# Decoder kernel on one core: zero matmuls between the products of the cosine stage, another order in a step, one bank for the sums

## The chip, the cores and the metric

The kernel runs on one core of a Trainium2 chip. A core has TensorE (PE: matmuls and weight loads), VectorE (DVE), ScalarE (ACT), GpSimd (POOL) and SyncE (SP, transfers). Each works through its own list of instructions in order and waits on semaphores that others raise. TensorE writes to PSUM, eight banks of 512 float columns; VectorE and ScalarE read them there. TensorE's clock is granted at one of two levels, 1.2 or 2.4 GHz; a profile shows it as 0.5 or 1.0. The metric is the device time of one execution in microseconds (us), smaller is better.

## What is computed

Two decoder layers on x of 16 sequences x 128 rows x 128 channels and a context of 16 x 128 x 96. Each part is added to x after a layer norm of x: in layer 0 causal attention, cross attention and a mixture of experts, in layer 1 attention over the batch, a cosine similarity with the context and an MLP with blockwise FP4 quantisation. The change touches the cosine part alone:

```python
def _L1_xattn_ref(visual_features, text_features, Wv, bv, Wt, bt):
    v = jnp.einsum('bsd,hd->bsh', visual_features, Wv) + bv      # h = 64
    t = jnp.einsum('bsd,hd->bsh', text_features, Wt) + bt
    dots = jnp.einsum('bih,bjh->bij', v, t)
    vn = jnp.linalg.norm(v, axis=-1)
    tn = jnp.linalg.norm(t, axis=-1)
    denom = jnp.maximum(vn[:, :, None] * tn[:, None, :], EPS)
    return dots / denom
...
    x = x + _L1_xattn_ref(_layernorm(x, axis=-1), ctx_768, L1_xattn_Wv, L1_xattn_bv, L1_xattn_Wt, L1_xattn_bt)
```

## The kernel before

The stages follow one another as blocks, with all engines meeting between two of them: the attentions of layer 0, the experts, the attention over the batch (`batch_attention`, from about 499 us), `back_block`, which turns its result back and adds it to x (670 to 681 us), `cosine_block` (682 to 722 us) and `mlp_block` (722 us to the end). x stays in SBUF all the time. The context's side of the cosine (`M.cos_tt`, the projected context, and `M.cos_inv`, its inverse norms) was made in an earlier stage.

`cosine_block` goes through the 16 sequences in pairs: N = 8 steps, u = 0 to 7, and p = u % 2 chooses one of two buffers. For a pair:

- VectorE subtracts the mean and scales (`normalise`, L1726, tile `cos_xn`).
- TensorE turns the two 128x128 tiles (`turn`, L1643); ScalarE copies them to SBUF (`turned`, L1695, `cos_xt`).
- TensorE multiplies with the weights (`project`, L1650, 64 x 256 result, recorded as two MATMULs of 256 columns). ScalarE squares it with the bias (`biased`, L1683, `cos_sq`) and stores it with the bias (L1685, `cos_vt`).
- TensorE sums the squares with a column of ones (`sums`, L1656: two matmuls of one column, recorded as four, each with its weight load). ScalarE takes the root (`roots`, L1690, `cos_norm`), VectorE floors it and takes the reciprocal (`inverses`, L1732 and L1735), GpSimd multiplies it into `M.cos_inv` and limits it (L1715, two tiles, `cos_m`).
- TensorE makes the products with the context (`products`, L1664: two matmuls of 128 columns, recorded as four). VectorE multiplies them by `cos_m` (`cosines`, L1740), adds the result to x (`add`, L1745) and takes the statistics for the next layer norm (`statistics`, L1751 and L1754).

The order is written by hand. In one pass of TensorE's loop over u stand `project` of pair u+1, `sums` and `products` of pair u and `turn` of pair u+2; ScalarE's passes are `biased` u+1, `roots` u, `turned` u+2; VectorE's are `normalise` u+3, `cosines` u-1, `inverses` u, `add` and `statistics` u-1. The loops are written out, not run on registers. `wait(engine, semaphore, u, per, plus)` waits until the semaphore has reached per * u + plus and is left out where that is zero or less. PSUM banks 0 and 1 hold the turned tiles, 2 and 3 the projections, 4 and 5 the sums, 6 and 7 the products, by parity.

The stage begins with the scales of the layer norm for all rows: VectorE adds the epsilon (L206), ScalarE loads its table and takes the root (L214), VectorE takes the reciprocal (L208).

Of the kernel before, what the change touches and what calls it, by code (L numbers as in the profile page):

```python
# [15 lines left out]
BF16 = mybir.dt.bfloat16  # L16
I32 = mybir.dt.int32
ALU = mybir.AluOpType
ACT = mybir.ActivationFunctionType
# [24 lines left out]
def wait(eng, sem, t, per=1, plus=0):  # L44


    value = per * t + plus
    if isinstance(value, int) and value <= 0:
        return
    eng.wait_ge(sem, value)  # L50
# [20 lines left out]
def valid(t, count):  # L71

    return not isinstance(t, int) or 0 <= t < count
# [35 lines left out]
def semaphores(nc, tag, names):  # L109


    return {n: nc.alloc_semaphore(name=f"{tag}_{n}") for n in names.split()}
# [92 lines left out]
def scales_on_vector(nc, M, dve, s):  # L205
    nc.vector.tensor_scalar(M.rstd[:, :, 0], M.mv[:, :, 1], EPS_LN, None, ALU.add).then_inc(s["variance"], 1)  # L206
    dve.wait_ge(s["root"], 1)
    nc.vector.reciprocal(M.rstd[:, :, 0], M.root[:, :]).then_inc(s["rstd"], 1)  # L208
    dve.wait_ge(s["rstd"], 1)


def scales_on_scalar(nc, M, act, s):
    act.wait_ge(s["variance"], 1)
    nc.scalar.activation(M.root[:, :], M.rstd[:, :, 0], ACT.Sqrt).then_inc(s["root"], 1)  # L214
# [1400 lines left out]
def cosine_block(nc, M, d):  # L1615
# [5 lines left out]
    with ExitStack() as ctx:  # L1621
        one = lambda n, shape, dt=F32: ctx.enter_context(nc.sbuf_tensor(f"cos_{n}", shape, dt))
        two = lambda n, shape, dt=F32: [one(f"{n}{p}", shape, dt) for p in range(2)]
        s = semaphores(nc, "cos", """variance root rstd xn xt_ps xt vt_ps vt sq sum_ps norm floored inverse
            limited dot_ps cosine x_done stats aggr""")
        N = B // 2
        xn, xt = two("xn", [S, 2, D]), two("xt", [D, 2, S])
        vt, sq = two("vt", [HC, 2, S]), two("sq", [HC, 2, S])
        norm, floored, inv = two("norm", [S, 2]), two("floored", [S, 2]), two("inv", [S, 2])
        m, cosine = two("m", [S, 2, S]), two("cosine", [S, 2, S])  # L1630
        stats = [one(f"stats{j}", [S, 6]) for j in range(4)]
        turn_bank, vt_bank, sum_bank, dot_bank = M.bank[0:2], M.bank[2:4], M.bank[4:6], M.bank[6:8]
        halves = lambda t: t[:, 0:2 * S].rearrange("p (j s) -> p j s", j=2)

        with nc.Block() as block:

            @block.tensor
            def _(pe):
                def turn(u, p):
                    wait(pe, s["xn"], u, per=2, plus=2)  # L1640
                    wait(pe, s["xt"], u, plus=-1)
                    for j in range(2):
                        mm = nc.tensor.transpose(turn_bank[p][:, j * S:(j + 1) * S], xn[p][:, j, :], M.ident[:, :])  # L1643
                    mm.then_inc(s["xt_ps"], 1)

                def project(u, p):
                    wait(pe, s["xt"], u, plus=1)
                    wait(pe, s["vt"], u, plus=-1)
                    wait(pe, s["sq"], u, plus=-1)
                    nc.tensor.matmul(vt_bank[p][0:HC, 0:2 * S], M.cos_wv[:, 0:HC], xt[p][:, :, :], start=True, stop=True).then_inc(s["vt_ps"], 1)  # L1650

                def sums(u, p):
                    wait(pe, s["sq"], u, plus=1)
                    wait(pe, s["norm"], u, plus=-1)
                    for j in range(2):
                        mm = nc.tensor.matmul(sum_bank[p][:, j:j + 1], sq[p][:, j, :], M.ones[0:HC, 0:1], start=True, stop=True)  # L1656
                    mm.then_inc(s["sum_ps"], 1)

                def products(u, p):
                    wait(pe, s["vt"], u, plus=1)  # L1660
                    wait(pe, s["cosine"], u, plus=-1)
                    for j in range(2):
                        b = 2 * u + j
                        mm = nc.tensor.matmul(dot_bank[p][:, j * S:(j + 1) * S], vt[p][:, j, :], M.cos_tt[:, b * S:(b + 1) * S], start=True, stop=True)  # L1664
                    mm.then_inc(s["dot_ps"], 1)

                for u in range(-2, N):
                    if valid(u + 1, N):
                        project(u + 1, (u + 1) % 2)
                    if valid(u, N):  # L1670
                        sums(u, u % 2)
                        products(u, u % 2)
                    if valid(u + 2, N):
                        turn(u + 2, u % 2)

            @block.scalar
            def _(act):
                scales_on_scalar(nc, M, act, s)

                def biased(u, p):  # L1680
                    wait(act, s["vt_ps"], u, plus=1)
                    wait(act, s["sum_ps"], u, plus=-1)
                    nc.scalar.activation(sq[p][:, :, :], halves(vt_bank[p][0:HC]), ACT.Square, bias=M.cos_bias[0:HC, 0:1]).then_inc(s["sq"], 1)  # L1683
                    wait(act, s["dot_ps"], u, plus=-1)
                    nc.scalar.activation(vt[p][:, :, :], halves(vt_bank[p][0:HC]), ACT.Identity, bias=M.cos_bias[0:HC, 0:1]).then_inc(s["vt"], 1)  # L1685

                def roots(u, p):
                    wait(act, s["sum_ps"], u, plus=1)
                    wait(act, s["floored"], u, plus=-1)
                    nc.scalar.activation(norm[p][:, :], sum_bank[p][:, 0:2], ACT.Sqrt).then_inc(s["norm"], 1)  # L1690

                def turned(u, p):
                    wait(act, s["xt_ps"], u, plus=1)
                    wait(act, s["vt_ps"], u, plus=-1)
                    nc.scalar.activation(xt[p][:, :, :], halves(turn_bank[p]), ACT.Copy).then_inc(s["xt"], 1)  # L1695

                for u in range(-2, N):
                    if valid(u + 1, N):
                        biased(u + 1, (u + 1) % 2)
                    if valid(u, N):  # L1700
                        roots(u, u % 2)
                    if valid(u + 2, N):
                        turned(u + 2, u % 2)
# [13 lines left out]

            @block.vector
            def _(dve):
                scales_on_vector(nc, M, dve, s)  # L1720

                def normalise(u, p):
# [328 lines left out]
def build(nc, d, out, stop=99):  # L2051
    M = Memory()
    with ExitStack() as ctx:
# [56 lines left out]
        if stop > 4:  # L2110
            cosine_block(nc, M, d)
# [79 lines left out]
```

## Time and profile before

| | |
|---|---|
| median of 3 runs | 806.65 us (806.61, 806.65, 810.84) |
| profiled execution | 807.06 us, its span 805.3 us |
| mean granted TensorE clock | 0.868 |
| busy share of the span | PE 77%, DVE 60%, PEld 57%, ACT 46%, POOL 29% |
| chain that ended last | DVE 7%, PE 1%, issue 1%: followed back through the last tenth only |
| cosine stage | about 682 to 722 us |

PE is TensorE's matmul side, PEld its weight loads, which run beside it. The busy shares are means over stages with different limits, so a stage is read from its own windows and its timeline. In a row of the timeline, "x2" says how many instructions were merged, and the brackets tell how long the engine had been idle before it and what it was waiting for. Matmuls are pipelined: the distance from one start to the next says more than the length of one. The time of the execution is 1.8 us longer than its span, which runs from the first to the last instruction.

### The profile page before, as it was taken

How to read it: one execution, taken by the hardware profiler on the slowest of the kernel's cores; microseconds unless marked ns; L12 is line 12 of the kernel's file. 1: busy time of each engine (PE TensorE's matmuls, PEld its weight loads, DVE VectorE, ACT ScalarE, POOL GpSimd, SP SyncE). 2: the span in 40 equal slices, each digit the busy share in tenths (PEclk: the TensorE clock that was granted, in tenths of full speed). 3: DMA queues.
4: the chain of work that ended last, by engine and by line, in shares of the span. 5: the costliest groups of instructions: out<-in, count | busy, mean ns of one | idle time of the engine just before them, and what ended most of it. 6: DMA issues, size and time to landing. Idle time of an engine off the chain costs nothing. (4 is left out here: it accounts for less than half of the span.)

```text
span 805.3 us, 16987 instructions
## 1 busy us (share of the span) xinstructions
PE 622.4 (77%) x6347; PEld 457.9 (57%) x6377; DVE 480.8 (60%) x1294; ACT 372.2 (46%) x801; POOL 234.0 (29%) x337
## 2 busy tenths in 40 slices
PE   4795999888999974356999913889999884875865
PEld 2453555555666543234998912667878773553554
DVE  2454554568878766742444336575756554458995
ACT  5472765768676722125444441634444423323432
POOL 3131222434444211761445560031313130230000
PEclk9898899999999995566999965999999997556797
DMA  3013243442212211115566441100000000000000
GB/s 98 2 31 90 56 105 104 108 113 71 56 38 73 68 39 48 51 55 172 202 211 213 170 105 31 53 2 2 2 2 2 2 2 1 1 0 1 13 15 26
DMA packets 53135, 48.95 MB, mean 61 GB/s; under 512 B 10331, under 2 KB 45645, under 8 KB 52797
## 3 DMA queue, kind: packets, MB, share of 16 engines
q1 hardware_dynamic: 47037, 41.09, 17.0%
q0 software_dynamic: 2496, 4.27, 1.7%
q10 hardware_dynamic: 3520, 2.50, 1.2%
q8 instruction: 51, 0.84, 0.4%
q14 instruction: 31, 0.25, 0.1%
HBM read 18.68 MB, written 15.54 MB: 42 GB/s over the span
## 5 line engine op out<-in xcount | busy, mean ns | idle before, releaser
L568 ACT ACTIVATE ptx<-bank 128x512 f32<-128x512 f32 x128 | 66.1, 602 | 99.4 <-PE bank L481 99.3
L1557 POOL COPY ptx<-over_pt 32x512 f32<-32x512 f32 x64 | 39.0, 610 | 138.6 <-DVE over_pt L1527 135.8
L1117 POOL DMA_INDIRECT results<-moe_y,moe_dest x46 | 45.3, 984 | 59.3 <-DVE moe_y L1254 51.4
L722 DVE SCALAR_TENSOR_TENSOR ptx<-ptx,bank 128x512 f32<-128x512 f32 x64 | 41.1, 684 | 25.2 <-PE bank L490 23.5
L707 DVE TENSOR_REDUCE l_m<-bank 128x4 f32<-128x512 f32 x64 | 40.9, 679 | 20.7 <-PE bank L465 20.7
L381 POOL TENSOR_TENSOR x<-x,l_back 128x128 f32<-128x128 f32 x32 | 14.6, 456 | 132.9 <-ACT l_back L581 121.8
L477 PE MATMUL bank<-ke 32*128 32x512 f32 x256 | 36.8, 641 | 19.4 <-issue 15.7
L1457 ACT ACTIVATE ke<-bank 64x512 f32<-64x512 f32 x64 | 38.0, 594 | 16.2 <-PE bank L1388 15.3
L681 DVE BATCH_NORM_STATS2 l_stats<-x 128x6 f32<-128x128 f32 x32 | 9.3, 291 | 54.6 <-POOL x L381 54.6
L707 DVE TENSOR_REDUCE l_m_raw<-bank 128x4 f32<-128x512 f32 x64 | 40.7, 674 | 0.1
L1112 POOL DMA_INDIRECT slots<-xs,moe_pos x32 | 32.3, 1010 | 28.6 <-DVE moe_pos L1197 18.6
L1431 PE MATMUL bank<-over_ot,over_wo 128*128 128x128 f32 x256 | 33.4, 285 | 6.1 <-DVE over_ot L1533 6.1
L1500 DVE COPY over_q<-bank 128x512 f32<-128x512 f32 x32 | 22.1, 691 | 24.7 <-PE bank L1388 24.7
L363 POOL TENSOR_TENSOR ke<-ke,heads 128x512 f32<-128x512 f32 x32 | 33.3, 1041 | 10.5 <-ACT ke L548 9.0
L508 PE MATMUL bank<-ptx,ke 128*32 128x128 f32 x1024 | 34.6, 276 | 2.3 <-DVE ptx L722 2.2
L1431 PEld LDWEIGHTS bank<-over_ot,over_wo 128*128 128x128 f32 x256 | 30.3, 194 | 8.1 <-DVE over_ot L1533 7.0
L508 PE MATMUL bank<-ptx,head_ones 128*32 128x128 f32 x1024 | 33.9, 273 | 0.0
L1040 ACT ACTIVATE moe_h<-bank,ptx 128x256 f32<-128x256 f32 x48 | 19.7, 471 | 28.6 <-PE bank L962 28.5
L727 DVE RECIPROCAL l_rden<-bank 128x128 f32<-128x128 f32 x32 | 30.4, 950 | 3.5 <-PE bank L508 3.5
L1421 PE MATMUL bank<-ptx,over_v 128*64 128x128 f32 x512 | 31.5, 276 | 0.0
L1421 PEld LDWEIGHTS bank<-ptx,over_v 128*64 128x64 f32 x512 | 27.6, 137 | 5.4 <-issue 4.8
L508 PEld LDWEIGHTS bank<-ptx,ke 128*32 128x32 f32 x1024 | 26.1, 109 | 7.1 <-issue 3.6
(344 smaller groups left out, 1636.0 us busy)
## 6 DMA issues: line engine op xcount, KB each, us to landing
slots<-blank SPq DMA_DIRECT2D x16, 528.0 KB, 4.7
ptx<-w SPq DMA_DIRECT2D x12, 578.0 KB
ke<-w SPq DMA_DIRECT2D x11, 578.0 KB, 3.3
w<-in_w SPq DMA_DIRECT2D x16, 256.0 KB
moe_xb<-slots SPq DMA_DIRECT2D x23, 132.0 KB
x<-in_x SPq DMA_DIRECT2D x4, 256.0 KB, 5.3
w<-results SPq DMA_DIRECT2D x4, 256.0 KB, 5.8
w<-results ACTq DMA_DIRECT2D x4, 256.0 KB, 5.6
```

What stands on the lines that cost most here:

```text
L363: nc.gpsimd.tensor_tensor(kxx[t % 2][:, :, :], front[(t - 3) % 4][:, 1, :].rearrange("p (a k) -> p a k", a=1).broadcast_to([128, 4, S]), M ...
L477: nc.tensor.matmul(score_bank[g][:, :], k[r, :], qxx[t % 4][r, :, :].rearrange("p j q -> p (j q)"), start=True, stop=False, skip_group_che ...
L508: mm = nc.tensor.matmul(pv_bank[32 * g:32 * g + 32, part * S:(part + 1) * S], w, probs[t % 2][:, g, j * S:(j + 1) * S], start=(j == 0), st ...
L568: nc.scalar.activation(probs[t % 2][:, g, :], score_bank[g][:, :], ACT.Exp, scale=SCALE0).then_inc(s["probs"], 1)
L707: nc.vector.tensor_reduce(mx[:, 4 * g:4 * g + 4], top_bank[g][:, :].rearrange("p (j k) -> p j k", j=4), AX.X, ALU.max, negate=True).then_i ...
L722: nc.vector.scalar_tensor_tensor(probs[t % 2][:, g, :], probs[t % 2][:, g, :], 1.0, floor_bank[g][:, :], ALU.min, ALU.max).then_inc(s["cli ...
L1112: nc.gpsimd.indirect_dma_start(M.slots, bass.IndirectOffsetOnAxis(pos[:, k, 4 * q + j:4 * q + j + 1], 0), M.xs[:, 4 * q + j, :], None).the ...
L1117: nc.gpsimd.indirect_dma_start(M.results, bass.IndirectOffsetOnAxis(dest[j % 4][:, n:n + 1], 0), y[j % 4][:, n, :], None, bounds_check=2 * ...
L1421: mm = nc.tensor.matmul(o_bank[r // 4][j:j + 64, r % 4 * S:(r % 4 + 1) * S], v[t % 3][:, h // 8, h % 8 * HB:(h % 8 + 1) * HB], ptx[t % 2][ ...
L1431: mm = nc.tensor.matmul(y_bank[:, 0:S], wo[:, r, :], ot[t % 2][:, r, :], start=r == 0, stop=r == PAIR - 1)
L1457: nc.scalar.activation(ke[h, r, j, :], ring[at_block(t, r, 1) % 3][h, :], ACT.Copy).then_inc(s["ke"], 1)
L1557: nc.gpsimd.tensor_copy(ptx[t % 2][r, :, r], pt[t % 2][r, :, :]).then_inc(s["spread"], 1)
```

## The change

- A tile `filler` (128x512, bf16) is set to zero by VectorE at the very start of the stage, ahead of the scales. `keep_busy(n)` waits for that and issues n matmuls of it with itself, 512 columns each, into bank 5, which nobody reads.
- A pass of TensorE's loop now begins with `turn` of pair u+2, then two fillers, `project` of pair u+1, two fillers, `sums` and `products` of pair u. The fillers stand in all ten passes, 40 in all, also where a pass has no turn or no projection.
- The sums of both parities lie in bank 4, columns 0:2 and 2:4. `sums` of pair u therefore waits until ScalarE has read the sums of pair u-1; before, it waited for those of pair u-2.

```diff
             """variance root rstd xn xt_ps xt vt_ps vt sq sum_ps norm floored inverse
-            limited dot_ps cosine x_done stats aggr""")
+            limited dot_ps cosine x_done stats aggr filler""")
...
-        turn_bank, vt_bank, sum_bank, dot_bank = M.bank[0:2], M.bank[2:4], M.bank[4:6], M.bank[6:8]
+        turn_bank, vt_bank, sum_bank, dot_bank, filler_bank = M.bank[0:2], M.bank[2:4], (M.bank[4][:, 0:2], M.bank[4][:, 2:4]), M.bank[6:8], M.bank[5]
+        filler = one("filler", [128, 512], BF16)
...
+                def keep_busy(n):
+                    pe.wait_ge(s["filler"], 1)
+                    for _ in range(n):
+                        nc.tensor.matmul(filler_bank[:, :], filler[:, 0:128], filler[:, :], start=True, stop=True)
...
                 def sums(u, p):
                     wait(pe, s["sq"], u, plus=1)
-                    wait(pe, s["norm"], u, plus=-1)
+                    wait(pe, s["norm"], u)
...
                 for u in range(-2, N):
+                    if valid(u + 2, N):
+                        turn(u + 2, u % 2)
+                    keep_busy(2)
                     if valid(u + 1, N):
                         project(u + 1, (u + 1) % 2)
+                    keep_busy(2)
                     if valid(u, N):
                         sums(u, u % 2)
                         products(u, u % 2)
-                    if valid(u + 2, N):
-                        turn(u + 2, u % 2)
...
             def _(dve):
+                nc.vector.memset(filler[:, :], 0.0).then_inc(s["filler"], 1)
                 scales_on_vector(nc, M, dve, s)
```

TensorE's list at the start of the stage, before. `ident` is the identity of a turn, `cos_wv` the weights of the projection:

```order
L1643 MATMUL bank<-ident,cos_xn 128x128 x2
L1650 MATMUL bank<-cos_xt,cos_wv 64x256
L1643 MATMUL bank<-ident,cos_xn 128x128 x2
L1650 MATMUL bank<-cos_xt,cos_wv 64x256
L1656 MATMUL bank<-ones,cos_sq 128x1 x2
L1664 MATMUL bank<-cos_tt,cos_vt 128x128 x2
```

The same place in the changed kernel:

```order
L1651 MATMUL bank<-ident,cos_xn 128x128 x2
L1645 MATMUL bank<-cos_filler 128x512 x4
L1651 MATMUL bank<-ident,cos_xn 128x128 x2
L1645 MATMUL bank<-cos_filler 128x512 x2
L1658 MATMUL bank<-cos_xt,cos_wv 64x256
L1645 MATMUL bank<-cos_filler 128x512 x2
L1651 MATMUL bank<-ident,cos_xn 128x128 x2
L1645 MATMUL bank<-cos_filler 128x512 x2
L1658 MATMUL bank<-cos_xt,cos_wv 64x256
L1645 MATMUL bank<-cos_filler 128x512 x2
```

The third turn and the second projection now stand ahead of the first sums, and twelve fillers do.

VectorE's list at the start of the stage in the changed kernel:

```order
L1728 UNCONDITIONAL_BRANCH
L1730 MEMSET cos_filler 128x256
L206 TENSOR_SCALAR rstd<-mv_a 128x16
L208 RECIPROCAL rstd<-root 128x16
L1737 TENSOR_SCALAR cos_xn<-x,mv_a,rstd 128x128 x8
```

The memset is the only new row there (the 512 half-width elements are written as 256 words); the scales and the first four pairs' normalised rows follow as before.

## Rows read from the trace of the kernel before

**Rows 1.** The page, TensorE's granted clock in 40 slices of 20.1 us, in tenths.
```profile
PEclk9898899999999995566999965999999997556797
```

**Rows 2.** Windows: stretch, length, busy us (instructions) of each engine, granted clock, DMA.
```profile
504.00:506.00 2.00, 2.00 (x9) 1.60 (x7) 0.82 (x2) 0.97 (x2) 0.00 (x0) 0.82 1.00 389
676.00:678.00 2.00, 0.33 (x2) 0.00 (x0) 1.88 (x12) 0.00 (x0) 0.00 (x0) 0.50 0.00 0
696.00:700.00 4.00, 3.71 (x12) 2.36 (x12) 2.26 (x10) 1.23 (x4) 1.31 (x3) 0.50 0.00 0
798.00:800.00 2.00, 1.91 (x8) 1.54 (x9) 0.12 (x1) 0.98 (x2) 0.00 (x0) 0.50 0.00 0
```

**Rows 3.** Timeline of one cosine step: start, length, engine, line, operation, idle before.
```profile
703.54 0.69 PE L1643 MATMUL bank<-ident,cos_xn 128*128 128x128 f32 x2
...
704.26 0.38 ACT L1695 ACTIVATE cos_xt<-bank 128x256 f32<-128x256 f32 x1 [1.51 <-PE bank L1643]
...
704.70 1.11 PE L1650 MATMUL bank<-cos_xt,cos_wv 128*64 128x256 f32 x2 [0.47 <-ACT cos_xt L1695]
...
705.74 1.01 PE L1656 MATMUL bank<-ones,cos_sq 64*128 64x1 f32 x4
...
706.62 1.20 PE L1664 MATMUL bank<-cos_tt,cos_vt 64*128 64x128 f32 x4
...
706.99 0.17 DVE L1732 TENSOR_SCALAR cos_floored<-cos_norm 128x2 f32<-128x2 f32 x1 [1.68 <-ACT cos_norm L1690]
...
707.46 1.61 POOL L1715 TENSOR_SCALAR cos_m<-cos_inv 128x128 f32<-128x128 f32 x2 [2.60 <-DVE cos_inv L1735]
...
707.75 0.69 PE L1643 MATMUL bank<-ident,cos_xn 128*128 128x128 f32 x2
```

**Rows 4.** Timeline, the start of the cosine stage.
```profile
681.92 1.28 ACT L214 ACT_TABLE_LOAD   x1 [6.22 <-PEq L1566]
...
684.41 0.69 PE L1643 MATMUL bank<-ident,cos_xn 128*128 128x128 f32 x2 [8.08 <-DVE cos_xn L1726]
...
690.37 0.17 DVE L1735 RECIPROCAL cos_inv<-cos_floored 128x2 f32<-128x2 f32 x1
```

**Rows 5.** Timeline, the end of the cosine stage, VectorE.
```profile
715.61 0.17 DVE L1735 RECIPROCAL cos_inv<-cos_floored 128x2 f32<-128x2 f32 x1
...
718.05 0.17 DVE L1735 RECIPROCAL cos_inv<-cos_floored 128x2 f32<-128x2 f32 x1
```

**Rows 6.** Timeline, TensorE, the start of the stage at 499 us.
```profile
499.60 0.76 PE L1386 MATMUL bank<-over_xhi,over_hi 128*128 128x512 f32 x1 [1.90 <-PEq L851]
...
504.00 0.63 PE L1387 MATMUL bank<-over_xlo,over_hi 128*128 128x512 f32 x1
504.43 0.54 PE L1388 MATMUL bank<-over_xhi,over_lo 128*128 128x512 f32 x1
```

**Rows 7.** Timeline, TensorE, bf16 matmuls of 512 columns in the first stage.
```profile
108.07 0.81 PE L457 MATMUL bank<-self_upper,self_identb 128*128 128x512 bf16 x3
108.81 1.14 PE L465 MATMUL bank<-ke 32*128 32x512 f32 x8
```

**Rows 8.** Timeline, TensorE, two stretches at full clock.
```profile
358.56 1.05 PE L947 MATMUL bank<-ones,ptx 64*128 64x1 f32 x8
359.54 1.07 PE L942 MATMUL bank<-ke,moe_cos_wt 96*64 96x512 f32 x2
...
382.65 0.38 PE L954 MATMUL bank<-ident,moe_xb 128*128 128x128 f32 x2
382.87 1.89 PE L962 MATMUL bank<-moe_xbt,ke 128*128 128x256 f32 x8
384.60 1.95 PE L974 MATMUL bank<-ptx,moe_h 128*128 128x128 f32 x16
```

**Rows 9.** Timeline, TensorE, the transposes of the stage before the cosine stage.
```profile
671.13 3.71 PE L1581 MATMUL bank<-ident,back_part 128*128 128x128 f32 x12 [1.23 <-ACT back_part L1572]
```

**Rows 10.** Groups by line and shape, VectorE: busy us, mean ns, idle before.
```profile
L1152 DVE MEMSET moe_zeros<- 128x512 f32 x1 | 0.5, 485 | 0.2 <-DVE moe_upto L1151 0.2
```

More of the change, by code:

```diff
@@ L1689, in roots @@
                     wait(act, s["floored"], u, plus=-1)
-                    nc.scalar.activation(norm[p][:, :], sum_bank[p][:, 0:2], ACT.Sqrt).then_inc(s["norm"], 1)
+                    nc.scalar.activation(norm[p][:, :], sum_bank[p], ACT.Sqrt).then_inc(s["norm"], 1)
                 def turned(u, p):
```

## The prediction, made before the changed kernel was run

> **What bounds the kernel now.** I read the page's clock line first, slices of 20.1 us: TensorE's granted clock reads 9 in the slices before 684 us and 5 in the two from 684 to 725 us, which are the cosine stage [rows 1]. The windows say the same in numbers: 0.50 in the window from 696 us to 700 us, with PE recorded busy 3.71 of 4.00 us, while DVE has 2.26, ACT 1.23 and POOL 1.31 [rows 2]. So the stage (about 682 to 722 us) is paced by TensorE at 1.2 GHz, one of its two levels. Next the timeline of one step [rows 3]. A step is 707.75 - 703.54 = 4.21 us, and TensorE issues all of it in series: the turn, then a hole until ScalarE has copied the turned rows (704.70 - 703.54 = 1.16, of it 0.47 idle "<-ACT cos_xt"), the projection 1.04, the sums 0.88, the products 1.13. VectorE stands idle 1.68 us in every step, until ACT has the norm, which comes from PE's sums; GpSimd stood idle 2.60. Nobody but TensorE is near its limit. Eight such steps lie on the path: the next stage takes its statistics from the last sum of this one. The page's chain covers only the last tenth of the span, so it decides nothing here.
>
> **The other engines' floor.** With TensorE out of the way two loops remain. VectorE's own work is 2.26 us in a 4.00 us window, so 2.38 a step. The other is reciprocal, two GpSimd multiplications, cosines, next reciprocal: the last step of before ran at exactly this pace, having no turn and no projection, 718.05 - 715.61 = 2.44 us [rows 5]. No step can be shorter than 2.44.
>
> **The change, part by part.**
>
> *Fillers, at half clock.* A filler streams 512 columns. The nearest rows at half clock are 512-column matmuls of the stage at 499 us, start to start 504.43 - 504.00 = 0.43 us [rows 6]. Four a step are 1.72.
>
> *Fillers, at full clock.* The one bf16 form with 512 columns in the trace ran at full clock, three of them in 108.81 - 108.07 = 0.74, so 0.25 each [rows 7]; four are 1.0.
>
> *The turn goes first.* At full clock two transposes take 382.87 - 382.65 = 0.22 [rows 8], at half I double it to 0.45. ScalarE's copy of the turned rows (0.38 plus hand-over) no longer stands between turn and projection: the projection of a step reads what was turned one step earlier. The 0.47 hole goes. What is late next is TensorE's own queue.
>
> *Does the clock rise?* This decides the sign. At the start of the stage before this one it rose after TensorE had streamed wide matmuls without a hole: it began at 499.60, the last long record starts at 504.43, and the clock of 504 to 506 us is 0.82 [rows 2, 6]. That is 4.9 us. The cosine stage of before has PE recorded busy nine tenths of the time and stays at 0.50 [rows 2]; its records are, however, partly one-column sums (0.88 us of weight loading per step with next to nothing streamed) and transposes. The changed stage starts differently: the order shows turn, four fillers, turn, two fillers, projection, two fillers, turn, two fillers, projection, two fillers, before the first one-column sum. None of these waits for anything that is late, so from 684.41 [rows 4] TensorE streams wide tiles without a hole for over 5 us. I take the rise at 684.41 + 4.9 = 689.3, and for the range 3 us to 8 us after the start. It then has four fillers a step to hold it up.
>
> *Against it.* Between 671 and 676 us TensorE did nothing but transposes, twelve of them recorded as 3.71 us without a hole, and in 676 to 678 us the clock is at 0.50 [rows 2, 9]. The Trainium skill, "TensorE: Matmul & The Clock Gate", section "Part 4: PE-mode transpose", has a rule for this: a transpose does not count as activity for the clock the way a matmul does. By that rule the turns (0.45 of a step at half clock) are holes; if fillers and products suffice all the same the sum below stands, if not it is the rival "cold". That fall agrees with the rule but does not prove it, since the engine also fell idle there.
>
> *First steps.* At half clock: 684.41 + turn 0.45 + four fillers 1.72 + turn 0.45 + two fillers 0.86 + projection 1.0 = 688.9; one filler more and the clock is up at 689.3. Then filler 0.25, turn 0.22, two fillers 0.5, projection 0.43 (eight 256-column records in 384.60 - 382.87 = 1.73, and it has two), two fillers 0.5, sums 0.49 (eight such records in 359.54 - 358.56 = 0.98, it has four) [rows 8]: 691.7. From the end of the sums to the floor is 706.99 - 706.62 = 0.4 for norm and hand-over [rows 3], and the floor with its hand-over takes 0.2, so the first reciprocal stands at 692.25, where before has it at 690.37 [rows 4]. The start loses 1.9 us.
>
> *A step at full clock.* 0.22 turn + 0.5 + 0.43 projection + 0.5 + 0.49 sums + 0.45 products (sixteen 128-column records in 1.95 with their tail, so about 0.11 each, four of them [rows 8]) = 2.6. I add 0.1 for waits and hand-overs: 2.7, above the floor of 2.44, below 4.21. Bounds: 2.44 and, if each of the six pieces lost 0.1, 3.2.
>
> *To the last reciprocal.* Steps 1 to 5 at 2.7 are 13.5, step 6 has no turn, 2.4, and step 7 has only the floor of 2.44: 692.25 + 18.35 = 710.6. Before has it at 718.05 [rows 5]. The stage gains 7.45 us. What follows (last multiplications, cosines, sum and statistics, to the stage's end near 722 us) is not TensorE's and stays as it is.
>
> *The memset ahead of the scales on VectorE.* A float memset of 128x512 took 0.485 us [rows 10]; this one has half the bytes. It delays the variance, but ScalarE is loading its table from 681.92 for 1.28 us [rows 4] and can't use the variance before 683.2. Cost zero; without that cover 0.3 to 0.5.
>
> *Sums of both parities in one bank.* The sums of step u now wait for the norm of u-1, read out of the bank. That norm is done less than 0.4 us after its sums (VectorE uses it at 706.99, the sums ended at 706.62) [rows 3]; the next sums start over 1.5 us later. Behind the wait stand the sums and products only. Zero; below nothing is excluded, since the edit frees only the bank for the fillers.
>
> *The next stage.* It starts with some 5 us in which TensorE has nothing to do, as before, so I expect it at half clock again. Its clock goes up and down several times [rows 1], and a stage that begins 7 us earlier meets other moments. Its last transposes and products ran at half clock (1.91 of 2.00 us busy at 0.50) [rows 2]. At the other level they would be shorter by up to 1.5 us; elsewhere as much can be lost. Plus or minus 1.5, nothing in the middle.
>
> **Sum.** The profiled execution took 807.06 us (span 805.3, 1.8 around it). 807.06 - 7.45 = 799.6. The median of the three runs shown is 806.65, 0.4 lower: forecast 799.2 us. The three runs spread to 810.84, so 0.5% (4 us, under 802.6 or over 810.7) is about what a measurement can tell from no change.
>
> **Rivals.**
> *Warm, but steps of 3.3 us*, from hand-overs that a shorter step uncovers (ScalarE has squares, values, norm, copy in one queue, and the norm now waits behind a projection's two activations). For: ScalarE's norm stands between PE and DVE in each step. Against: ACT is busy 1.23 of 4.00 us. Five steps of 0.6 more are 3.0: 802.2 us.
> *Late rise*: the clock stays at half for some steps. A step at half clock is 0.45 + 0.86 + 1.0 + 0.86 + 0.87 + 1.13 = 5.2 us, 2.5 more than a warm one. Two such steps leave 2.5 us of gain, 804 us; three leave none.
> *Cold, the slower side*: the sums, the turns and zero operands keep the activity too low and the clock never rises. The first reciprocal comes at 694.4, then five steps of 5.2, one of 4.7 and one of 3.7 (four fillers, sums, products of the last step): 728.7, that is 10.7 later than 718.05, so 817.3 us. For: busy records alone did not raise it in this stage. Against: the opening stretch without sums, and 1.72 us of wide tiles in each step. It decides from three cold steps of the eight on.
> *No effect* (fillers warm the clock, but TensorE did not pace the stage) is ruled out by VectorE's and GpSimd's idle rows, other than as the late rise.
>
> **Chances.** Forecast 0.70 (796 to 802, with the rise, the step length and the next stage's phase in it); steps of 3.3 us 0.11; late rise 0.08; cold 0.11. The range 796.0 to 804.5 holds the first three nearly whole and leaves out the cold case and a little at the low end. Faster by over 0.5%: all of the forecast and over half of the 3.3 us case, 0.77. Slower: the cold case, 0.11. The rest, 0.12, is within 0.5%.
>
> **What would show it.** Right: granted clock 0.50 until about 689 us and 1.00 from there to the end of the stage; cosine steps of 2.6 to 2.8 us; no idle time before the projection; VectorE's wait for the norm down from 1.68 to under 0.3 us; the start's first reciprocal some 2 us later than before. Wrong: clock 0.50 in the middle of the stage, steps over 5 us, ScalarE idle behind the fillers. A warm stage with a gain under 4 us would say that the step's length was mis-sized; a gain in the stage that the end doesn't show would point to the clock of the next stage.

## The result

Against the kernel before, run on the same chip, the changed kernel takes 800.27 us (median; 799.48 to 802.75) where before takes 808.49 (806.61 to 810.84). The ratio is 0.9909, 95% interval 0.9886 to 0.9932, so 0.7 to 1.1% faster. The forecast was 799.2 us from a before of 806.65; the difference forecast was 7.45 us. The medians lie 8.2 us apart, and the ratio makes it 7.4. A second series beside the later experiments gave 801.59 us against 807.48 (ratio 0.9918, 0.9887 to 0.9948).

The profiled execution took 799.48 us with a span of 797.7, 7.6 less than before's 805.3. The page's clock line, to be held against [rows 1]:

```profile
PEclk9898899999999995556999975899999999796787
```

Windows of the changed kernel (columns as in [rows 2]):

```profile
684.00:688.00 4.00, 3.78 (x11) 1.54 (x10) 1.29 (x5) 0.38 (x1) 0.00 (x0) 0.50 0.00 0
688.00:692.00 4.00, 4.00 (x22) 2.10 (x22) 0.49 (x3) 2.38 (x7) 0.04 (x1) 0.98 0.01 4
696.00:700.00 4.00, 3.84 (x22) 2.11 (x22) 3.00 (x13) 2.08 (x6) 2.24 (x3) 1.00 0.00 0
```

The clock is at 0.50 when the stage begins and at 1.00 from about 688 us. From there TensorE is recorded busy nearly all the time. One step at full clock, to be read beside [rows 3]:

```profile
697.72 0.44 PE L1651 MATMUL bank<-ident,cos_xn 128*128 128x128 f32 x2
...
698.00 0.59 PE L1645 MATMUL bank<-cos_filler 128*128 128x512 bf16 x2
...
698.52 0.19 PEld L1658 LDWEIGHTS bank<-cos_xt,cos_wv 128*64 128x64 f32 x2 [0.42 <-issue]
698.52 0.65 PE L1658 MATMUL bank<-cos_xt,cos_wv 128*64 128x256 f32 x2
...
699.10 0.61 PE L1645 MATMUL bank<-cos_filler 128*128 128x512 bf16 x2
...
699.63 0.60 PE L1664 MATMUL bank<-ones,cos_sq 64*128 64x1 f32 x4
...
700.10 0.69 PE L1672 MATMUL bank<-cos_tt,cos_vt 64*128 64x128 f32 x4
...
700.48 0.17 DVE L1743 TENSOR_SCALAR cos_floored<-cos_norm 128x2 f32<-128x2 f32 x1 [0.38 <-ACT cos_norm L1700]
...
700.72 0.44 PE L1651 MATMUL bank<-ident,cos_xn 128*128 128x128 f32 x2
```

A step is 700.72 - 697.72 = 3.00 us instead of 4.21. The hole before the projection is gone and no wait for another engine stands in its place on TensorE. VectorE still waits for the norm, 0.38 us instead of 1.68. The start of the stage, beside [rows 4]:

```profile
681.14 1.28 ACT L214 ACT_TABLE_LOAD   x1 [6.22 <-PEq L1566]
681.25 0.27 DVE L1730 MEMSET cos_filler<- 128x256 uint32 x1 [1.00 <-PEq L1566]
...
683.62 0.69 PE L1651 MATMUL bank<-ident,cos_xn 128*128 128x128 f32 x2 [8.01 <-DVE cos_xn L1737]
...
691.68 0.17 DVE L1746 RECIPROCAL cos_inv<-cos_floored 128x2 f32<-128x2 f32 x1
```

From first turn to first reciprocal 8.06 us pass instead of 690.37 - 684.41 = 5.96, so the start loses 2.10. The memset took 0.27 us under the table load, as forecast. The end, beside [rows 5]:

```profile
711.85 0.17 DVE L1746 RECIPROCAL cos_inv<-cos_floored 128x2 f32<-128x2 f32 x1
...
715.90 1.41 PE L1879 MATMUL bank<-ident,wq_q 128*128 128x128 f32 x6 [4.32 <-PEq L1636]
```

From the first turn to the last reciprocal the stage takes 28.23 us, before 33.64. That is 5.41 of the 7.6. The rest is in two other places. The first turn itself comes 0.79 earlier. That is scatter: over the thirteen profiles of this study, three of them of kernels with other code ahead of it, it lies anywhere between 683.6 and 689.7 us, while from the last product of the batch attention to the first turn 14.8 us pass in all thirteen. The first matmul of that attention already starts anywhere between 499.1 and 503.9 us. The MLP stage is 1.4 us shorter, 0.9 of it in its first 12 us: to the second product of gate and up it takes 726.96 - 715.90 = 11.06 us in the changed kernel,

```profile
726.96 0.52 DVE L1996 TENSOR_TENSOR mlp_h<-mlp_g,bank 128x352 f32<-128x352 f32 x1 [1.27 <-ACT mlp_g L1954]
```

and 734.09 - 722.10 = 11.99 before, where VectorE waited 1.82 us there instead of 1.27:

```profile
734.09 0.52 DVE L1985 TENSOR_TENSOR mlp_h<-mlp_g,bank 128x352 f32<-128x352 f32 x1 [1.82 <-ACT mlp_g L1943]
```

The windows from 9 to 11 us after that stage's first matmul, the changed kernel first and then before, show what differs there:

```profile
724.90:726.90 2.00, 1.75 (x6) 0.88 (x4) 0.52 (x1) 0.67 (x3) 0.00 (x0) 0.79 0.00 0
```

```profile
731.10:733.10 2.00, 2.00 (x5) 1.14 (x4) 0.52 (x1) 0.46 (x1) 0.00 (x0) 0.50 0.00 0
```

By the 0.79 TensorE's clock rises 9.8 us after the stage begins in the changed kernel. In the kernel before it is still at 0.50 here and rises 11.3 us after the stage begins, so 1.5 us later.

### The profile page after: what moved, and what is told of

Same layout as the page of the kernel before. It is cut to its first block and busy times, and to the rows that moved or that the text cites. A ratio compares the mean times of both kernels' runs of the same rounds, so it can differ in the third digit from the quotient of the medians.

```text
span 797.7 us, 17066 instructions
## 1 busy us (share of the span) xinstructions
PE 616.7 (77%) x6384; PEld 451.5 (57%) x6417; DVE 480.2 (60%) x1295; ACT 371.2 (47%) x801; POOL 233.7 (29%) x337
```

## The experiments

Each kernel was compared with before on the same chip. "Stage" is the time from the first turn to the last reciprocal in the kernel's profile. The first four shared a chip and a series of before (median 808.43).

### The order without the fillers

```diff
                 for u in range(-2, N):
                     if valid(u + 2, N):
                         turn(u + 2, u % 2)
-                    keep_busy(2)
                     if valid(u + 1, N):
                         project(u + 1, (u + 1) % 2)
-                    keep_busy(2)
```

> The changed kernel without its 40 fillers: only the turn goes first and the sums share a bank. Stage time is counted from the first turn to the last reciprocal: 33.6 us before, 28.2 us changed. Theory A (the clock brought the gain): the clock stays at 0.50 and the step keeps nearly all of its 4.21 us; the stage takes 31 to 33 us and the kernel is at most 2 us faster than before. Theory B (the order brought it): the hole before the projection goes and at half clock the step is 0.45 + 1.05 + 0.88 + 1.13 = 3.5 us, the stage about 29 us, the kernel some 4.5 us faster than before. Adding the pieces from the trace speaks for B in the step's length, so 3.5 us is what I expect, with the clock at 0.50 throughout.

Measured: 804.39 us, ratio 0.9936 (0.9915 to 0.9958); stage 29.78 us, step 3.67. Timeline of a step and a window of this kernel:

```profile
701.23 0.69 PE L1651 MATMUL bank<-ident,cos_xn 128*128 128x128 f32 x2
...
701.84 1.12 PE L1658 MATMUL bank<-cos_xt,cos_wv 128*64 128x256 f32 x2
...
702.89 1.01 PE L1664 MATMUL bank<-ones,cos_sq 64*128 64x1 f32 x4
...
703.77 1.20 PE L1672 MATMUL bank<-cos_tt,cos_vt 64*128 64x128 f32 x4
...
704.89 0.69 PE L1651 MATMUL bank<-ident,cos_xn 128*128 128x128 f32 x2
```

```profile
696.00:700.00 4.00, 4.00 (x15) 2.69 (x15) 2.27 (x10) 1.61 (x6) 1.60 (x2) 0.50 0.01 4
```

The clock stays at 0.50, and the pieces are 0.61 + 1.05 + 0.88 + 1.12. Theory B was right: the order alone shortens the stage by 3.86 us, without any fast clock. With the fillers and the clock on top it is 5.41, so they add 1.55 to it. That is what they add behind the order, and not what they are worth alone, as the next run shows.

### The fillers without the order

```diff
                 for u in range(-2, N):
-                    if valid(u + 2, N):
-                        turn(u + 2, u % 2)
-                    keep_busy(2)
                     if valid(u + 1, N):
                         project(u + 1, (u + 1) % 2)
                     keep_busy(2)
                     if valid(u, N):
                         sums(u, u % 2)
                         products(u, u % 2)
+                    if valid(u + 2, N):
+                        turn(u + 2, u % 2)
+                    keep_busy(2)
```

> The fillers without the new order: projection, two fillers, sums, products, turn, two fillers. Theory A: the clock rises as in the changed kernel (0.50 until about 5 us after the first turn, then 1.00) and the fillers behind the turn cover ScalarE's copy, so the step is the same 3.0 us and the kernel as fast as the changed one. Theory B (the order is needed): a hole stays before the projection, the step is over 3.3 us.

Measured: 800.80 us, ratio 0.9901 (0.9877 to 0.9925); step 3.11, stage 27.63. Here the fillers behind the turn cover ScalarE's copy up to a rest of about 0.1 us:

```profile
697.21 0.59 PE L1645 MATMUL bank<-cos_filler 128*128 128x512 bf16 x2
...
697.85 0.19 PEld L1658 LDWEIGHTS bank<-cos_xt,cos_wv 128*64 128x64 f32 x2 [0.54 <-ACT cos_xt L1705]
```

So either edit alone removes most of the hole, and their gains don't add up: the order alone gives the stage 3.86 us, the fillers alone 6.01, both together 5.41. With the fillers in place the new order shortens the step by 0.11 us and lengthens the start. The stage is 0.6 shorter here than in the changed kernel because its first reciprocal comes 6.52 us after the first turn instead of 8.06: between the first turn and the first sums stand eight fillers and one more turn, where the changed kernel has twelve and two more, and the clock rose 3.7 us after the first turn instead of 4.6. In the total the two can't be told apart.

### Half the fillers

```diff
-                    keep_busy(2)
+                    keep_busy(1)
...
-                    keep_busy(2)
+                    keep_busy(1)
```

> One filler instead of two at each place, 20 in all. At full clock a pair of fillers took 0.52 us of the changed kernel's step of 3.00 and TensorE never stood idle. If the clock rises all the same, the step is 3.0 - 0.5 = 2.5 us, the stage some 3 us shorter than in the changed kernel. If two fillers a step don't raise it, the step is at half clock 3.5 + 0.86 = 4.4 us and the kernel is slower than before.

Measured: 799.19 us, ratio 0.9888 (0.9862 to 0.9914); step 2.57, stage 24.28, 3.95 shorter than in the changed kernel. The clock rises and holds:

```profile
698.13 0.17 DVE L1743 TENSOR_SCALAR cos_floored<-cos_norm 128x2 f32<-128x2 f32 x1
```

```profile
700.00:704.00 4.00, 4.00 (x25) 2.60 (x25) 3.32 (x16) 2.21 (x8) 2.16 (x4) 1.00 0.00 0
```

VectorE's floor has no idle time ahead of it any more. TensorE has none either, 4.00 of 4.00 us, and its pieces add up to the 2.57, so it still paces the step, by a hair: without fillers in the steps (the next run) the step at full clock is 2.52, which is the loop of VectorE and GpSimd. The 3.95 us are gained in the stage; the spans of the two profiles differ by 1.3 us only, since the first turn came 3.0 us later in this one, and the medians by 1.1, with intervals that overlap, so the total doesn't show it clearly.

### Fillers only until the first sums

```diff
-                    keep_busy(2)
+                    keep_busy(2 if u < 1 else 0)
...
-                    keep_busy(2)
+                    keep_busy(2 if u < 1 else 0)
```

> Fillers only in the first three passes of TensorE's loop (12 of them, up to the first sums), none after. Theory A1: the stage's own work is enough to hold the clock up once it is up; TensorE's work in a step is then about 2.0 us, the step falls to the floor of GpSimd's loop, 2.45 us, and the stage is about 3 us shorter than in the changed kernel. Theory A2: the fillers are needed to hold it; the clock falls back to 0.50 within two or three steps and the step becomes 3.5 us, the stage about as long as without fillers.

Measured: 800.89 us, ratio 0.9913 (0.9885 to 0.9941); stage 26.67, steps 2.37, 2.52, 2.52, 2.52, 3.52, 3.04, 2.44.

```profile
692.00:696.00 4.00, 4.00 (x25) 2.64 (x24) 2.54 (x12) 2.30 (x8) 2.83 (x4) 1.00 0.02 4
696.00:700.00 4.00, 3.58 (x16) 1.89 (x15) 3.59 (x18) 1.20 (x5) 2.40 (x3) 0.74 0.00 0
700.00:704.00 4.00, 4.00 (x15) 2.69 (x15) 2.76 (x13) 1.61 (x6) 2.31 (x3) 0.50 0.00 0
```

```profile
698.18 0.69 PE L1651 MATMUL bank<-ident,cos_xn 128*128 128x128 f32 x2 [0.42 <-DVE cos_xn L1737]
```

The clock held for some steps and then fell, with PE recorded busy 4.00 of 4.00 us in the window ahead. The fall came at about 697.95, in TensorE's first longer hole, 0.42 us in which it waited for VectorE's next rows. Such a hole alone doesn't explain it: the kernel with the gap filled, below, kept the clock at 1.00 through holes of up to 1.04 us with matmuls between them. So the stage's own work (turns, projections, one-column sums with their weight loads, short products) doesn't hold the clock here. Theory A2 is right, though the fall came later than I had put it. To hold the clock the fillers inside the steps are needed, one at each place is enough. For the stage's time two at each place are worse than none behind the first sums: this one is 1.56 us shorter than the changed kernel's, though its clock fell.

### Transposes as fillers

```diff
-        filler = one("filler", [128, 512], BF16)
+        filler = one("filler", [128, 128])
...
-                    for _ in range(n):
-                        nc.tensor.matmul(filler_bank[:, :], filler[:, 0:128], filler[:, :], start=True, stop=True)
+                    for _ in range(2 * n):
+                        nc.tensor.transpose(filler_bank[:, 0:128], filler[:, :], M.ident[:, :])
```

> The changed kernel with each 512-column filler replaced by two float transposes of a zero tile, which stream for the same time (0.21 us each at half clock by the turns' rows). The Trainium skill, page TensorE: Matmul & The Clock Gate, section Part 4: PE-mode transpose, says that a transpose does not count as activity for the clock. Theory R (by that rule, as a mechanism of this kernel): the clock stays at 0.50 in the stage, the step is 3.67 (what the order alone gave) + 4 x 0.43 = 5.4 us and the kernel 5 us or more slower than before. Theory C (they count like matmuls): the clock rises about 5 us after the first turn, the step is 3.0 us, the time that of the changed kernel.

Measured: 801.93 us against 807.02, ratio 0.9929 (0.9911 to 0.9946); step 3.05, stage 28.60. The windows and two groups of fillers:

```profile
689.70:693.70 4.00, 4.00 (x17) 3.54 (x18) 1.64 (x6) 0.38 (x1) 0.00 (x0) 0.50 0.01 4
693.70:697.70 4.00, 4.00 (x26) 2.65 (x24) 0.16 (x1) 2.29 (x7) 0.00 (x0) 0.94 0.00 0
702.00:706.00 4.00, 4.00 (x28) 2.77 (x26) 2.95 (x14) 1.90 (x6) 2.35 (x3) 1.00 0.00 0
```

```profile
692.29 1.06 PE L1645 MATMUL bank<-ident,cos_filler 128*128 128x128 f32 x4
...
695.00 0.60 PE L1645 MATMUL bank<-ident,cos_filler 128*128 128x128 f32 x4
```

In the first 3.6 us TensorE did nothing but transposes, then one projection, 1.0 us long, at 0.50. The clock rose within that projection, 4.5 us after the first turn as in the changed kernel, and four transposes went from 0.99 to 0.53 us. So here float transposes did what matmuls did. The Trainium skill ("TensorE: Matmul & The Clock Gate", Part 4: PE-mode transpose) says that the fast clock doesn't engage for transposes; in this kernel the measurement decides against it. What made the clock fall in the kernel before, in a stage with transposes [rows 9], is then open. It did not wait for TensorE to fall idle:

```profile
674.00:676.00 2.00, 1.56 (x7) 0.93 (x7) 1.88 (x13) 1.70 (x6) 0.00 (x0) 0.85 0.01 4
```

By the 0.85 it fell at about 675.4, while the last four transposes ran (675.28 to 676.33). They were thinly spread, though: the twelve before them took 3.71 us at full clock, 0.31 each, where four took 0.53 here, 0.13 each. With matmuls put among them, as in the next run, the clock stayed up. Whether the spacing alone decides wasn't tried.

### TensorE busy ahead of the stage

This kernel, on top of half the fillers, streams identity matmuls in the stage before and four fillers ahead of the first turn:

```diff
+def stream(nc, M, bank, n):
+    for _ in range(n):
+        nc.tensor.matmul(bank[:, 0:128], M.ident[:, :], M.ident[:, :], start=True, stop=True)
...
                     mm.then_inc(s["y_ps"], 1)
+                    if not (isinstance(q, int) and q == 0):
+                        stream(nc, M, M.bank[7], 4)
                 both(pe, N, four)
+                stream(nc, M, M.bank[7], 6)
...
+                keep_busy(4)
                 for u in range(-2, N):
```

> One filler at each place, and TensorE kept streaming before the stage: identity matmuls behind the later groups of transposes of the stage before, and four fillers ahead of the first turn. With half the fillers the first reciprocal came 6.57 us after the first turn, 5.96 before the change, because the first passes ran at half clock. Theory: the clock is up when the stage starts, the first reciprocal comes 4.5 us after the first turn, the steps stay at 2.57 us, the stage is 2 us shorter than with half fillers alone (24.3), the kernel near 797 us. Rival: the streaming ahead delays the stage before or its end, and the first turn comes later by as much.

Measured: 798.35 us against 807.02, ratio 0.9890 (0.9867 to 0.9914); stage 24.28, first reciprocal 6.57 us after the first turn, both as with half the fillers alone.

```profile
676.00:680.00 4.00, 4.00 (x39) 4.00 (x38) 3.76 (x24) 1.79 (x6) 0.00 (x0) 1.00 0.01 2
680.00:684.00 4.00, 0.57 (x6) 0.38 (x4) 2.89 (x20) 0.03 (x1) 0.00 (x0) 0.90 0.00 0
684.00:688.00 4.00, 3.03 (x8) 1.45 (x10) 2.27 (x9) 1.85 (x3) 0.00 (x0) 0.50 0.02 6
```

The clock was held through the stage before, but between 680 and 684 us, across the meeting of the engines, TensorE had 0.57 us of work, and at the first turn it was back at 0.50. My theory fell. The rival didn't hold either: from the last product of the batch attention to the first turn it took 14.8 us as in every other kernel, so nothing came later. There was just no effect.

### The MLP stage

On top of that, in the MLP stage TensorE streams where it waits for VectorE, paced by VectorE's own steps:

```diff
                 def turn(u, p):
+                    if isinstance(u, int) and u == N - 1:
+                        for k in range(1, SIGNED_STEPS):
+                            pe.wait_ge(s["step"], SIGNED_STEPS * u + k)
+                            stream(nc, M, row_bank, 2)
                     wait(pe, s["step"], u, per=SIGNED_STEPS, plus=SIGNED_STEPS)
...
                 pe.wait_ge(s["clear"], 2)
+                for k in range(1, SIGNED_STEPS):
+                    pe.wait_ge(s["row_step"], k)
+                    stream(nc, M, y_bank, 1)
                 pe.wait_ge(s["weights"], 3)
```

> As the warm start, and in the MLP stage TensorE streams identity matmuls in two places where it waits for VectorE: beside the first row quantisation and beside the last hidden quantisation, one or two after each of VectorE's steps. The last transposes and products took 794.5 - 790.3 = 4.2 us at half clock in the changed kernel, where before also had them at half. Theory: at full clock they take 2.3 us, and the first products of the stage are 1 to 2 us shorter: 2 to 4 us less than the warm start. Rival: VectorE's time in between sets the stage, the head's gain is swallowed, and only the tail's 2 us stay.

Measured: 793.47 us against 807.02, ratio 0.9834 (0.9811 to 0.9858). The MLP stage takes 78.6 us, with the warm start alone 81.4. The second product of gate and up, the last transposes and the last sum of this kernel, and the same three with the warm start alone:

```profile
722.20 0.52 DVE L2012 TENSOR_TENSOR mlp_h<-mlp_g,bank 128x352 f32<-128x352 f32 x1 [0.19 <-ACT mlp_g L1970]
...
785.57 0.87 PE L1922 MATMUL bank<-ident,mlp_hq 128*128 128x128 f32 x6 [0.22 <-DVE mlp_hq L1842]
...
788.46 0.42 DVE L2043 TENSOR_TENSOR x<-x,bank 128x256 f32<-128x256 f32 x1 [2.62 <-PE bank L1930]
```

```profile
725.60 0.52 DVE L2005 TENSOR_TENSOR mlp_h<-mlp_g,bank 128x352 f32<-128x352 f32 x1 [1.02 <-ACT mlp_g L1963]
...
788.97 1.54 PE L1918 MATMUL bank<-ident,mlp_hq 128*128 128x128 f32 x6 [4.47 <-DVE mlp_hq L1842]
...
793.07 0.42 DVE L2036 TENSOR_TENSOR x<-x,bank 128x256 f32<-128x256 f32 x1 [3.83 <-PE bank L1926]
```

From the transposes to the sum 2.89 us pass instead of 4.10, which is 1.21 of the 2.8. The first matmul of the stage stands at 713.01 here and at 714.78 with the warm start alone, so to the second product of gate and up it takes 9.19 us instead of 10.82. That is the rest, 1.63. The rival, that VectorE swallows the head's gain, didn't hold.

### The bank alone

```diff
-        turn_bank, vt_bank, sum_bank, dot_bank = M.bank[0:2], M.bank[2:4], M.bank[4:6], M.bank[6:8]
+        turn_bank, vt_bank, sum_bank, dot_bank = M.bank[0:2], M.bank[2:4], (M.bank[4][:, 0:2], M.bank[4][:, 2:4]), M.bank[6:8]
...
-                    wait(pe, s["norm"], u, plus=-1)
+                    wait(pe, s["norm"], u)
```

> The kernel before with the sums of both parities in one bank and the wait for the norm of the step before, nothing else. I expect no effect: the step stays at 4.21 us, the stage at 33.6 us. Rival: the wait for the norm holds TensorE's sums back and the step grows by 0.2 us or more.

One run, 808.34 us. The stage is 33.64 us as before, and so is the step:

```profile
704.93 0.17 DVE L1735 RECIPROCAL cos_inv<-cos_floored 128x2 f32<-128x2 f32 x1
...
709.13 0.17 DVE L1735 RECIPROCAL cos_inv<-cos_floored 128x2 f32<-128x2 f32 x1
```

The shared bank and its wait cost nothing at this length of a step. In the changed kernel's shorter step TensorE waited for no other engine between its pieces either.

### The MLP's streaming without the warm start, the gap filled, the changed kernel again

The first has half the fillers and the MLP's edits only. The second is the kernel with all three, and these lines more:

```diff
                 both(pe, N, four)
                 stream(nc, M, M.bank[7], 6)
+                pe.wait_ge(s["x_done"], N)
+                stream(nc, M, M.bank[7], 2)
+                pe.wait_ge(s["stats"], 4 * N)
+                stream(nc, M, M.bank[7], 2)
...
-                keep_busy(4)
+                stream(nc, M, filler_bank, 4)
+                pe.wait_ge(s["root"], 1)
+                stream(nc, M, filler_bank, 2)
                 for u in range(-2, N):
```

> One filler at each place and the streaming in the MLP stage, but nothing ahead of the cosine stage. The warm start had brought nothing in the cosine stage (first reciprocal 6.57 us after the first turn with it and without it), so I expect this to equal the kernel with all three, 793.5 us: cosine stage 24.3 us, MLP stage 78.6 us against 81.4 with half fillers alone. Rival: the streaming ahead did matter for the MLP stage, by the moment at which the clock rises there, and this one is 1 us or more slower.

> All three, with the gap ahead of the cosine stage filled: identity matmuls also beside VectorE's last work of the stage before, and six more between the start of the block and the root, without waiting for the zero tile. In the warm start TensorE stood idle for 4.2 us there and the clock was back at 0.50 when the first turn came. Theory: with no gap over 1.5 us the clock is 1.00 at the first turn, the first reciprocal comes 4.5 us after it instead of 6.57, the kernel is 2 us faster than the one with the gap, near 791.5 us. Rival: the clock falls all the same and nothing changes, or the MLP stage gives the 2 us back because its clock now rises at another moment.

> The changed kernel once more, beside these. In the single profiles the MLP stage took 81.4 to 81.8 us in the kernels whose cosine stage ended at full clock and 82.4 to 83.2 in those where it ended at half. If that is a property of the kernel and not of the run, this profile has 81.4 to 82.0 us again, the step is 3.00 us, the stage 28.2, the median within 1 us of 800.3. If it is chance, the MLP stage differs by over 0.7 us from 81.8.

Measured, against 807.48 us: without the warm start 793.96 us, ratio 0.9828 (0.9802 to 0.9855), cosine stage 24.30, MLP stage 78.3. It equals the kernel with all three; the early streaming was useless as it stood.

With the gap filled: 793.13 us, ratio 0.9819 (0.9793 to 0.9845), cosine stage 22.72, MLP stage 78.3.

```profile
680.00:684.00 4.00, 2.62 (x18) 2.08 (x19) 1.80 (x12) 1.50 (x2) 0.00 (x0) 1.00 0.00 2
684.00:688.00 4.00, 3.52 (x17) 1.59 (x18) 1.46 (x6) 1.93 (x6) 0.00 (x0) 1.00 0.00 0
```

```profile
683.80 0.44 PE L1663 MATMUL bank<-ident,cos_xn 128*128 128x128 f32 x2 [0.21 <-DVE cos_xn L1752]
...
688.81 0.17 DVE L1761 RECIPROCAL cos_inv<-cos_floored 128x2 f32<-128x2 f32 x1
```

The clock is at 1.00 from the first turn on, and the first reciprocal comes 5.01 us after it instead of 6.57; I had put 4.5. So the mechanism holds and the stage is 1.6 us shorter, but the medians of the two kernels are only 0.8 us apart, inside what the runs scatter. This is the fastest kernel of the study, 1.8% faster than before; that it beats the one without the early streaming is shown in the profile's stage only.

The changed kernel again: step 3.00, stage 27.81, MLP stage 81.4 us. The stage is 0.42 shorter than the first time. The clock rose 3.7 us after the first turn instead of 4.6, and 0.9 us of TensorE's work at twice the pace is worth 0.45. The MLP stage is within the expected 81.4 to 82.0, so the shorter one seems to belong to the kernel. Over all profiles without the MLP's edits it takes 82.4 to 83.2 us where the cosine stage ended at half clock (before, one bank, order only, fillers until the first sums) and 81.4 to 81.8 where it ended at full clock (the other six). The two groups differ in when the clock first rises in that stage, too: 9.3 to 9.8 us after its first matmul in the six and 10.4 to 11.3 in the four. With TensorE streaming there it rises after 3.4 to 6.0 us, and the stage takes 78.3 to 78.6. So the stage's length goes with the moment of its own rise. Why that moment should hang on how the cosine stage ended wasn't tried.

## Why the prediction was right, point by point

**The total** was right, 799.2 forecast and 800.27 measured, inside the range. It was partly luck: the cosine stage gained 5.41 us instead of 7.45, which the MLP stage and scatter made good in the profile, with 1.4 and 0.79. For the MLP stage I had put plus or minus 1.5 and nothing in the middle.

**What bounds the stage**: right. TensorE at half clock, with the hole before the projection. My reading of the clock line was loose: of the slices before 684 us the last one reads 7 and not 9 [rows 1], since the clock fell at 675.4. The floor was nearly right: the last step took 2.43 or 2.44 in every kernel, but it is no bound for all of them. With fillers only until the first sums one step took 2.37, in which GpSimd's two multiplications are recorded as 1.53 us, and the next three 2.52, with 1.69 in each; in the last step of before they are 1.61.

**The rise of the clock**: right. Forecast at 689.3, 4.9 us after the first turn; the windows show it between 684 and 688 at 0.50 and from 688 to 692 at 0.98, so some 4.5 us after the first turn at 683.62. Over all kernels whose clock rose in this stage it was 3.5 to 4.6 us.

**The first steps**: 1.9 us lost by the sum, 2.10 measured, and 1.67 in the second profile of the kernel.

**A step at full clock**: this term was mis-sized, 2.7 forecast, 3.00 measured in all five full steps. Piece by piece from the timeline: turn 0.28 (0.22 forecast), fillers 0.52 and 0.53 (0.5), projection 0.58 (0.43), sums 0.47 (0.49), products 0.62 (0.45). The bound of 3.2 held. The step lies halfway to the rival of 3.3, but not for the rival's reason: TensorE waited for no other engine. I had taken the spacings from long rows of equal instructions [rows 8]; here the weights change their shape after every second or fourth record. Taken record by record, a change of shape costs some 0.09 us. The last filler before the projection (the timeline narrowed to that moment) stands at 698.21, 0.31 ahead of the projection at 698.52:

```profile
698.21 0.38 PE L1645 MATMUL bank<-cos_filler 128*128 128x512 bf16 x1
```

Two fillers start 0.22 apart, which is why one alone took 0.30 in the run with half of them and two took 0.52. There are four such changes in a step: fillers to projection, projection to fillers, fillers to sums, products to turn. Where the shape stays, from turn to fillers and from sums to products, the next record starts 0.11 after the last, as inside a row. At the four changes the profile has the next weight load starting only with its own matmul (0.42 us "issue" in the PEld row of the step above); elsewhere it starts ahead of it. So the changes cost 0.37 a step, and three smaller gaps inside turn, projection and products 0.05 to 0.08 each. My lump for all hand-overs was 0.1, and my 0.25 for a filler held a part of the rest. That the late load is the cause is read from where the two coincide; no run changed the shapes. Five steps of 0.3, 0.34 in step 6 and 0.2 at the start are the 2.04 us that are missing.

**The hole before the projection**: right that it goes and that TensorE's own queue is next. What I did not work out is what the order alone is worth. I treated the clock as what decides the sign. The order alone gave 3.86 us of the stage at half clock and the kernel was 0.6% faster without any fast clock. At half clock this kernel's own fillers would have turned that into a loss, by an estimate of 3.67 + 4 x 0.43 = 5.4 us a step. Nor did I work out that fillers behind the turn remove the hole without the new order. The cold rival (5.2 us a step) was not met by any run, since every kernel with fillers in its steps got the fast clock.

**The rule on transposes**: I had left it as a condition of the cold rival. The run with transposes as fillers shows the opposite of what the Trainium skill says in the section cited there, with the clock at 1.00 in the stage. I had also set down that the engine fell idle where the clock fell near 676 us; the window of 674 to 676 us, given with that run, shows the fall before the transposes had ended.

**The memset and the bank**: zero each, as forecast; the bank by a run of its own at half clock, the memset by its row under the table load.

**The next stage**: it does start at half clock again, as forecast. That it would be shorter in both profiles of the kernel was not foreseen.

**The signs**: of those listed two were missed, the steps (3.00 us, not 2.6 to 2.8) and VectorE's wait for the norm (0.38, not under 0.3).

## What to carry to other kernels

Zero matmuls in TensorE's waits bring the fast clock and hold it, but their number is to be tried: here half of them brought it just as well and left the steps within 0.05 us of the other engines' loop. Before paying for a clock, look for the hole in the order: a turn put one place earlier gave 3.86 us of the stage with no filler at all. And test each of two edits alone: the fillers without the new order gave more than both together. And take a step's length from rows with the same change of shapes, not from long runs of one shape.

## What was not expected of the hardware

- PE recorded busy 4.00 of 4.00 us is no sign of a fast clock: with turns, projections, one-column sums and short products alone it stayed at 0.50 with 4.00 of 4.00, and brought to 1.00 it fell back after four steps.
- Float transposes of a zero tile raised the clock just as matmuls did, 4.5 us after the first turn.
- At full clock a change in the shape of the weights cost some 0.09 us between two matmuls.
- Between two blocks, with 0.57 us of TensorE work from 680 to 684 us, the clock went from 1.00 to 0.50; with ten small matmuls placed across the same gap it was at 1.00 at the first turn.
- A kernel whose cosine stage ends at full clock has an MLP stage about 1 us shorter, though TensorE is at half clock when that stage begins. Its clock then rises 9.3 to 9.8 us after the first matmul instead of 10.4 to 11.3; why is open.
- The first turn came anywhere within 6 us from profile to profile, and 4.8 of them stood before the batch attention began, so stages, not totals, tell a gain of 2 us.
